# The last two expert tiles by halves of the experts, with the next layer's norm and transposes between them

## The reference

```python
gate = jax.nn.softmax(y @ gate_W + gate_b, axis=-1)
hid = jax.nn.gelu(jnp.einsum('bnd,edf->bnef', y, W1) + b1)
eo = jnp.einsum('bnef,efd->bned', hid, W2) + b2
out = jnp.einsum('bned,bne->bnd', eo, gate)
...
xn = _layernorm(x, axis=-1)
x = x + _L1_gnn_ref(xn, ...) + _L1_mix_ref(xn[None], ...)[0]
```

## Time and profile before

| | |
|---|---|
| device time, three runs | 2430.15 us median (2429.15 to 2435.55) |
| the profiled execution | 2428.97 us, span 2427.2 us |
| mean granted clock of PE | 0.939 |
| PE, DVE, ACT, POOL busy | 2166.4, 1320.5, 732.4, 832.8 us |
| the chain that ended last | PE 62%, DVE 15%, POOL 10%, ACT 5%, issue 5%, DMA 3% |
| expert stage's outputs end | 2016.24 us |
| logits of the second layer begin | 2033.30 us |

### The profile page before, as it was taken

The page is one execution under the profiler, slowest core; times in us unless marked ns, Lnnn a source line. Parts: engine busy times, 40 slices in busy tenths (PEclk is TensorE's granted clock), DMA queues, the critical chain, the costliest instruction groups (busy, mean ns, idle before and its releaser), DMA issues.

```text
span 2427.2 us, 31743 instructions
## 1 busy us (share of the span) xinstructions
PE 2166.4 (89%) x11604; PEld 1264.2 (52%) x11604; DVE 1320.5 (54%) x4053; ACT 732.4 (30%) x1620; POOL 832.8 (34%) x648
## 2 busy tenths in 40 slices
PE   3999976899797899998899999998999998989975
PEld 2455544444332444444676447666866664455553
DVE  4555577577994566665222553343022225259997
ACT  4111111222001444443222335555411111034452
POOL 2018888788786655665000000000000000013442
PEclk9998877899898899999999998999999999999986
DMA  9992222222323867765300002000300005000000
GB/s 362 419 361 3 3 3 3 4 4 4 55 3 41 235 167 184 186 170 143 118 1 10 1 19 87 1 1 24 116 1 1 1 1 127 16 1 9 10 10 18
DMA packets 87071, 177.28 MB, mean 73 GB/s; under 512 B 64674, under 2 KB 65661, under 8 KB 70812
## 3 DMA queue, kind: packets, MB, share of 16 engines
q1 hardware_dynamic: 41169, 173.38, 22.1%
q0 software_dynamic: 45072, 1.46, 5.8%
q10 hardware_dynamic: 674, 0.39, 0.1%
HBM read 106.88 MB, written 68.31 MB: 72 GB/s over the span
## 4 chain that ended last, share of the span: by engine, by line
PE 62%; DVE 15%; POOL 10%; ACT 5%; issue 5%; DMA 3%; SPq 0%; DVEq 0%; ACTq 0%; POOLq 0%
PE banks L197 18%; POOL edge_table L537 7%; PE banks L2131 6%; PE banks L2171 6%; PE banks L1495 3%; PE banks L1313 3%; PE banks L354 2%; PE banks L1326 2%; PE banks L191 2%; PE banks L1967 2%; DMA edge_table<-arena 2%; PE banks L1940 2%; PE banks L1954 2%; POOL arena L1263 2%; PE banks L2553 2%
## 5 line engine op out<-in xcount | busy, mean ns | idle before, releaser
L197 PE MATMUL banks<-arena 128*125 128x512 f32 x1200 | 561.3, 615 | 17.6 <-DVE arena L2773 15.2
L537 POOL DMA_INDIRECT edge_table<-arena x313 | 489.0, 1562 | 241.4 <-DMA edge_table<-arena 147.1
L197 PEld LDWEIGHTS banks<-arena 128*125 128x125 f32 x1200 | 223.5, 194 | 293.1 <-issue 267.3
L1231 DVE TENSOR_TENSOR arena<-banks,arena 125x500 f32<-125x500 f32 x200 | 208.5, 1052 | 143.0 <-ACT banks L1290 106.0
L1263 POOL TENSOR_TENSOR arena<-arena 125x500 f32<-125x500 f32 x180 | 222.5, 1246 | 141.0 <-DVE arena L1231 135.3
L2580 POOL CAST arena<-arena 125x128 f32<-125x128 uint32 x10 | 2.9, 290 | 719.2 <-DVE arena L2716 719.2
L1313 PE MATMUL banks<-arena 64*125 64x250 f32 x800 | 141.7, 432 | 35.8 <-DVE arena L1231 29.4
L2079 DVE SCALAR_TENSOR_TENSOR arena<-banks,arena 125x512 f32<-125x512 f32 x80 | 60.1, 751 | 189.4 <-PE banks L2171 189.4
L1290 ACT ACTIVATE banks<-banks 125x500 f32<-125x500 f32 x200 | 114.5, 573 | 159.6 <-PE banks L1316 159.2
L2131 PEld LDWEIGHTS banks<-arena 128*128 128x128 f32 x1280 | 144.0, 192 | 6.7 <-issue 6.6
L2131 PE MATMUL banks<-arena 128*128 128x125 f32 x1280 | 146.4, 276 | 0.1
(11 more groups left out here) (353 smaller groups left out, 3553.0 us busy)
## 6 DMA issues: line engine op xcount, KB each, us to landing
edge_table<-arena SPq DMA_DIRECT2D x24, 2250.0 KB, 37.0
arena<-edge_table SPq DMA_DIRECT2D x50, 984.4 KB
arena<-L_ffn_W SPq DMA_DIRECT2D x4, 2048.0 KB, 11.1
arena<-edge_table SPq DMA_DIRECT2D x50, 114.3 KB
adjacency<-arena SPq DMA_DIRECT2D x50, 109.4 KB
arena<-adjacency SPq DMA_DIRECT2D x10, 546.9 KB
edge_table<-arena POOLq DMA_INDIRECT x313
arena<-x SPq DMA_DIRECT2D x1, 2240.0 KB
```

Of the source, the lines that this page charges most:

```text
L197: last = nc.tensor.matmul(dst, xT[:, i, :], w[:, i, 0:n], start=(i == 0), stop=(i == k - 1))
L537: pool.indirect_dma_start(d["table"], bass.IndirectOffsetOnAxis(ap=cell[0:EP, c:c + 1].bitcast(U32), axis=0), vals[0:EP, c * ROW:(c + 1) * ...
L1231: nc.vector.tensor_tensor(P_g[n % PRING][0:TP, :].rearrange("p (e n) -> p e n", e=2), two_scores(n), ring[(c * TILES + b) % RING][0:TP, :, ...
```

## The change

The outputs of the expert stage follow a list `OUTS`: tiles 0 to 7 as before, then experts 0 to 3 of tile 8, 0 to 3 of tile 9, 4 to 7 of tile 8, 4 to 7 of tile 9. With that, `w2_e[0]` is free when the second halves begin. DVE sums the degrees and takes their root in tile 8's first half, aggregates tiles 0 to 7 and takes their root in tile 9's first half, and normalizes one row of tiles 0 to 7 after each expert of the second halves; tiles 8 and 9 get a root and normalized rows of their own at the end. PE turns rows 0 to 5 one by one after the last six outputs, then rows 6 and 7, then projects H of tiles 0 and 1, then turns rows 8 and 9, which use banks 2 and 3. All this is ahead of the barrier. In the second layer's stage PE begins with the logits, DVE scales H of tiles 0 and 1 first and adds the bias to `X` in four pieces of 2, 3, 3 and 2 rows, and ACT begins with an exponential of one element. Seven projections stand in the rounds as before, and one follows.

```diff
         def inverse_root_dve(dve, src, eps):
-
-            steps["var"] += 1
-            nc.vector.tensor_scalar(var_eps[0:TP, :], src, eps, None, ALU.add).then_inc(s_var, 1)
...
+            root_begun(src, eps)
+            root_ended(dve)
@@ before the expert stage
+        EARLY = TILES - 2
+        OUTS = [(t, e) for t in range(EARLY) for e in range(EXPERTS)]
+        for half in range(2):
+            OUTS += [(t, e) for t in (EARLY, EARLY + 1) for e in range(EXPERTS // 2 * half, EXPERTS // 2 * (half + 1))]
...
@@ expert_dve
+            for q, (t, e) in enumerate(OUTS):
...
+                if e == 0 and 1 <= t <= EARLY:
+                    dve.wait_ge(e_x, tile_done[t - 1])
+                    link(dve, gather_stats(X, t - 1))
+                if (t, e) == (EARLY, 1):
+                    by_part_deg = degree_parts[0:TP, 0:TILES * CHUNKS].rearrange("p (t c) -> p t c", c=CHUNKS)
+                    link(dve, nc.vector.tensor_reduce(dinv[0:TP, :], by_part_deg, AX_X, ALU.add))
+                    root_begun(dinv[0:TP, :], 1.0)
+                if (t, e) == (EARLY, 3):
+                    root_ended(dve)
+                    nc.vector.tensor_copy(dinv[0:TP, :], rstd[0:TP, :])
+                    link(dve, nc.vector.tensor_tensor(root[0:TP, :], var_eps[0:TP, :], rstd[0:TP, :], ALU.mult))
+                if (t, e) == (EARLY + 1, 0):
+                    for u in range(EARLY):
+                        last = nc.vector.bn_aggr(mv[0:TP, u, :], bn6[0:TP, u, :])
+                    link(dve, last)
+                    root_begun(mv[0:TP, first, 1], 1e-5, first)
+                if (t, e) == (EARLY + 1, 3):
+                    root_ended(dve, first)
+                if e >= EXPERTS // 2 and t >= EARLY:
+                    u = EXPERTS // 2 * (t - EARLY) + e - EXPERTS // 2
+                    normalize(XN[0:TP, u, :], X[0:TP, u, :], u).then_inc(s_xn, 1)
...
+            for t in range(EARLY, TILES):
+                normalize(XN[0:TP, t, :], X[0:TP, t, :], t).then_inc(s_xn, 1)
             leave_stage(dve, "DVE")
@@ expert_act
+            ln_stats_act(act)
+            ln_stats_act(act, slice(0, EARLY))
+            for t in range(EARLY):
+                turned_row(act, t)
+            ln_stats_act(act, slice(EARLY, TILES))
+            for t in range(EARLY, TILES):
+                turned_row(act, t)
             leave_stage(act, "ACT")
@@ expert_pe
+            for q, (t, e) in enumerate(OUTS):
...
+                pe.wait_ge(e_a, NH // 4 * t + e // 2 + 1)
+                if q >= 3:
+                    pe.wait_ge(e_x, out_added[OUTS[q - 3]])
...
+                if q >= len(OUTS) - EARLY + 2:
+                    turn_row(pe, q - (len(OUTS) - EARLY + 2))
+            for t in range(EARLY - 2, EARLY):
+                turn_row(pe, t)
+            pe.wait_ge(s_wn, 16 * 9)
+            for t in range(2):
+                pe.wait_ge(n_zT, EARLY - 1 + t)
+                project_h(t)
+            for t in range(EARLY, TILES):
+                turn_row(pe, t)
             leave_stage(pe, "PE")
@@ l1_dve
-            ln_stats_dve(dve, X, 1e-5, gathered=True)
-            for t in range(TILES):
-                normalize(XN[0:TP, t, :], X[0:TP, t, :], t).then_inc(s_xn, 1)
...
-            fillers = iter(range(TILES))
+            fillers = iter(range(2, TILES))
+            for t in range(2):
+                scale_h(t)
...
+                if r == 0:
+                    add_bias(range(0, 2))
                 dve.wait_ge(o_pe, at + 3)
...
+                if r == 0:
+                    add_bias(range(2, 5))
                 scale_h(next(fillers))
@@ l1_act
-            ln_stats_act(act)
-
-            for t in range(TILES):
-                turned_row(act, t)
-            ln_stats_act(act)
+            nc.scalar.activation(st_n[0:1, 7:8], ones[0:1, 0:1], ACT.Exp)
@@ l1_pe
-            for t in range(TILES):
-                turn_row(pe, t)
             pe.wait_ge(n_zT, TILES)
-            fillers = iter(range(TILES))
-            pe.wait_ge(o_dve, 1)
+            fillers = iter(range(2, TILES))
```

More of the change, by code:

```diff
@@ L2070, in expert_dve @@
             dve.wait_ge(e_gate, 4)
-            for t in range(TILES):
+            first, late = slice(0, EARLY), slice(EARLY, TILES)
+            for q, (t, e) in enumerate(OUTS):
                 x = X[0:TP, t, :]
[L2073 to L2085, removed]
@@ L2154, in expert_pe @@
             pe.wait_ge(e_gate, 6)
-            for t in range(TILES):
[L2156 to L2173, removed]
+            for q, (t, e) in enumerate(OUTS):
+                if e == 0:
+                    if t >= 1:
+                        pe.wait_ge(e_x, bias_added[t - 1])
+                    nc.tensor.matmul(bank(1)[0:TP, :], gateT[0:EXPERTS, 128 * t:128 * t + TP], b2_e[0:EXPERTS, :],
+                                     start=True, stop=True).then_inc(e_b, 1)
+                    if t >= 1 and t + 1 < TILES:
+                        for a in range(NH // 4):
+                            expert_hidden(pe, t + 1, a)
+                pe.wait_ge(e_a, NH // 4 * t + e // 2 + 1)
+                if q >= 3:
+                    pe.wait_ge(e_x, out_added[OUTS[q - 3]])
+                for c in range(2):
+                    last = nc.tensor.matmul(bank(5 + q % 3)[0:TP, :], hT_e[t % 2][:, 2 * e + c, :],
+                                            w2_e[e // 4][:, 2 * (e % 4) + c, :], start=(c == 0), stop=(c == 1))
+                last.then_inc(e_o, 1)
+                if q >= len(OUTS) - EARLY + 2:
+                    turn_row(pe, q - (len(OUTS) - EARLY + 2))
@@ L2362, in l1_dve, with add_bias @@
                                     ALU.mult)
-            for t in range(TILES):
-                last = nc.vector.tensor_tensor(X[0:TP, t, :], X[0:TP, t, :], bias_n[0:TP, :], ALU.add)
-            link(dve, last)
+            def add_bias(tiles):
+                for t in tiles:
+                    last = nc.vector.tensor_tensor(X[0:TP, t, :], X[0:TP, t, :], bias_n[0:TP, :], ALU.add)
+                link(dve, last)
             def scale_h(t):
@@ L2481, in l1_pe @@
                     last.then_inc(o_pe, 1)
+                if r == 0:
+                    pe.wait_ge(o_dve, 1)
                 for j, (a, b) in enumerate(CH):
```

71 lines of the change are left out of this document (48 added, 23 removed).

## The result

| | before | after |
|---|---|---|
| device time, 15 runs each | 2431.13 us median (2426.26 to 2438.28) | 2422.68 us median (2414.87 to 2426.20) |
| ratio | | 0.996, 95% interval 0.9949 to 0.997 |
| span of the profiled execution | 2427.2 | 2420.9 |
| tile 8's bias product to the first neighbours | 141.10 | 129.92 |
| logits of the second layer begin | 2033.30 | 2033.24 |

The kernel is 8.45 us faster by the medians, 0.35%, and the interval of the ratio leaves out 1; its upper end, 0.997, is just the 0.3% that a measurement can tell from no change. The forecast was 2418.5 in 2413.5 to 2423.0: the point is 4.2 us low, and the range holds the time by only 0.3 us. With single times from 2414.87 to 2426.20, on which side of that end the median came to lie was partly luck. One of these 4.2 is the kernel before, whose median over 15 runs is 1.0 above that of the first three.

A forecast was written before the change was run, and what follows sets the result against it. Bound: VectorE, ScalarE, VectorE between last expert output and logits, TensorE on both sides. 6.16 + 2.81 + 2.99 + 1.64 - 0.6 - 0.3 - 1.0 = 11.7 us less: 2417.3 profiled, 2418.5 median; range 2413.5 to 2423.

The forecast's parts named there:

- Order of the halves: Expert outputs of tiles 8 and 9 reordered as 8a, 9a, 8b, 9b: cost 0, or 0.3 and 0.1 us without bank room.
- Transposes: Ahead of the logits: the 6.16 us hole goes, ten transposes take 5.10 for 7.91, less 0.6 for weight switches.
- The wait ahead of row 7: TensorE, after transposes 5 and 6, waits 0.3 us for VectorE to normalize row 7.
- Two projections and the late root: Ahead of the last transposes, transpose 7 and two projections cover the root of tile 9: slack 3.9 us, cost 0.
- The second hole: TensorE's 2.99 us hole ahead of the second layer's logits goes; copy of row 9, handing over and barrier take 1.0.
- The clock: First round's logits and strip sums in the second layer return to full clock: 1.64 us saved, bounds 0 and 1.64.
- The bias additions: The 6.11 us on VectorE, cut into four pieces, fit its first-round waits: cost 0, uncovered up to 6.1 us.
- The adjacency: Load behind the barrier takes 31.3 us; VectorE gets a new 4.5 us wait at the diagonal, slack 2.2, cost 0.
- The Exp table load: Moved to the head of the second layer on ScalarE, ahead of the logits' copies: 1.28 us, cost 0.
- a lost piece of clock: Rival, chance 0.15: a dip at the barrier gives back 1.64 us and half a projection more: 2420.2 to 2422.
- The rival of the falling clock in the interleaved stretch: Chance 0.04: low clock from the first transpose between experts; a loss if over 11.7 us of work, up to 2441.
- The late adjacency: Rival, chance 0.08: transfers past 33.5 us cost one for one at the maxima; 20% slower costs 4.1: 2422.6.

## Why the prediction was right, and where it was off

By its steps:

- *Order of the halves, cost 0*: right. The outputs run without a gap. I had not asked what the order gains; it is 0.7.
- *Transposes*: the hole is gone and ten transposes cost less than I said. A pair of an expert and a transpose takes 2.15 (2011.72 to 2013.87), an expert alone 1.73 (seven from 1999.60 to 2011.72), so a transpose between experts costs 0.42, not 0.51 + 0.10. The term for the switches of weights, 0.6, was mis-sized: nothing of it is seen, and some 0.5 more was saved (0.09 each for those between experts), 1.1 together.
- *The wait ahead of row 7*: 0.60 for 0.3. The row was there 1.3 us behind the outputs' end, as forecast (2022.62 to 2023.93); but TensorE needed only 0.9 for the two transposes, not 1.1, and 0.15 went by between the row's end and the transpose.
- *Two projections and the late root*: right; VectorE had rows 8 and 9 at 2027.5, 3.9 ahead of their transposes at 2031.40. That is the slack forecast.
- *The second hole*: 0.82 for 1.0. *The clock*: 1.64 came back whole; 1.00 in all windows from 1992 to 2058.
- *The bias additions*: cost 0, right, and 6.9 without the cut, near the 6.1 that I gave as the price uncovered, though by another sum.
- *The adjacency*: wait 4.8 for 4.5, load 32.3 for 31.3, slack 2.9 for 2.2, cost 0. Right in each part, and shown from both sides.
- *The Exp table load*: the exponential starts 0.02 behind the load, and the strip sums are on time. The Trainium skill, ScalarE: Activation LUTs, section What ACT_TABLE_LOAD costs, adds a drain to a switch; neither this row nor the forecast's has it. ScalarE's timeline of the changed kernel:

```profile
2033.19 1.28 ACT L2482 ACT_TABLE_LOAD   x1
2034.49 0.20 ACT L2482 ACTIVATE arena<-arena 1x1 f32<-1x1 f32 x1
```

The mechanism held in each part that was forecast. The step that failed is the one that takes the rest as unchanged, "what is saved ahead of the logits moves all that follows". The dip behind the folding product is 1.7 longer than before. As a rival I had a lost piece of clock at 0.15, but put it at the barrier and called a vanishing dip equally likely. The stretch then balances: 11.7 forecast, plus 1.1 and 0.2 on switches and barrier, less 0.3 at row 7 and 1.7 in the dip, is 11.0, and 11.2 and 11.0 were measured. Behind the stretch 0.6 is lost, which leaves 10.4 to 10.6 as the change's worth. The medians said 8.45 with 15 runs and 10.2 with 8; with single times that spread over 10 us, much of it from the edge table's stage, the missing 2 us of the first are most likely scatter. No run shows that by itself.

The rival of the falling clock in the interleaved stretch is out: 1.00 in every window from 1998 to 2032, with a transpose behind each of six outputs. The Trainium skill, TensorE: Matmul & The Clock Gate, Part 4, says that a transpose doesn't count as busy; here no dip came from them, with the clock at 1.00 throughout. The late adjacency and the change without effect are out as well.

## What to carry to other kernels

A filler can be worth more than the wait that it covers: here TensorE's holes of 2.5 to 4.4 us were each paid again in clock behind them, with 1.6 us (the hole of 2.99 in the kernel before) to 3.1 in the variants made for it, and 3.2 came back when the last one was filled. When a barrier moves, look up what the queues start behind it; a wait that it creates is free up to its slack, and one experiment that delays it by a known amount checks the slack that the trace shows. And compare traces by a stretch between two fixed operations: it repeated to 0.15 us where the whole time scattered by over 10.

## What was not expected of the hardware

- TensorE's clock falls during 32 back-to-back matmuls of eight columns: no gap, and 0.57 on the mean in the 8 us that begin with their second half. In ten traces this group and the projection behind it take 10.7 to 10.8 us, in the two of the kernel before 9.11. At full clock it would be some 7.3, an estimate: 3.74, with the clock high to its end, and 3.60 for a projection.
- The clock can rise while nothing but transposes runs: from 0.50 in 2022.4 to 2026.0 to 0.85 on the mean in the next 4.3 us.
- A transpose (four matmuls of 125 columns in float32) between output groups costs 0.42 us, with no sign of a cost for the change of weights.
- The adjacency and the output weights (7.3 MB: ten times 625 KB and 1.05 MB) take 32.1 to 32.3 us whether they start at the barrier or 7.8 us behind it, 226 GB/s on the mean, with the DMA share at about 1.0.
